# Scores of two 16-head attentions contracted over 32 rows instead of 128, with one copy of the keys

## The chip, the cores and the metric

One core of a Trainium2 chip runs the whole kernel in one launch. The metric is device microseconds (us) of one execution; the profile beside it is one execution taken by the hardware profiler. Engines are called by their short names: PE is TensorE (matmuls; PEld is its weight loads), DVE is VectorE, ACT is ScalarE, POOL is GpSimd, SP issues the DMAs.

## What is computed

Two layers of a small perceiver-like model on x of 4 batch elements, 128 tokens, 128 channels, all in float32. The change touches only the two attentions with 16 heads of 8 channels. The first reads keys from a context of 2048 tokens, of which each head sees every sixteenth, so 128; the second attends over x itself with a relative bias:

```python
# L0_xattn: TK = 2048, head h sees the keys k with (k - h) % 16 == 0, so 128 of them
scores = einsum('bhqd,bhkd->bhqk', Q, K) / sqrt(8)
scores = where((kidx - head) % 16 != 0, -inf, scores)
out = einsum('bhqk,bhkd->bhqd', softmax(scores), V) @ Wo.T + bo
# L1_attn: 128 queries, 128 keys, 16 heads
scores = einsum('bhqd,bhkd->bhqk', q, k) * 8 ** -0.5 + bias(rel. position, head)
out = einsum('bhqk,bhkd->bhqd', softmax(scores), v) @ w_proj.T + b_proj
```

Between them stand a selective-scan layer, a quantised gated MLP, and an attention over the context; behind the second a quantised MLP. Each is preceded by a layer norm and added to x.

## The kernel before, in words

The program is written engine by engine; every engine runs its own fixed list of instructions in order and waits on semaphores. `attention(ph)` stands once in each of the PE, ACT and DVE lists, with ph = 0 for the first 16-head attention and ph = 1 for the second. It is a software pipeline over steps t. In the first 16 steps, step t works on batch element b = t // 4 and on head group g = t % 4 (4 heads each), and one PE bank of PSUM (banks 0 to 2 in turn) holds the 128 queries by 4 x 128 keys of scores.

The channels of q and k lie on the 128 partitions: group g on rows 32g to 32g + 31, and in it head j on 8 rows. PE's score matmuls (L1197 to L1199, recorded at L1089, the helper `mm`) have as stationary operand `q_heads[:, j, ...]`, in which DVE (`queries`, L735 and L738) has multiplied the queries by a mask that keeps the 8 rows of head j in every group. The moving operand is `k_groups[:, g, ...]`: a copy of the keys in which only the 32 rows of group g hold something and the others are zero. So all 128 rows are contracted, and the zeros pick the group. DVE zeroes all of `k_groups` at the start (L857). ACT fills it: `keys(v)` (L431) and `self_keys(b)` (L465) issue four activations of 32 rows for each batch element, one for each group. At the very first batch element each group's copy releases its own step (`k_first`).

One float32 matmul of these is two passes on PE (two records in the trace), a float32 transposition is one. In step t, PE issues: the 4 score matmuls of step t (8 passes of 128 rows by 128 columns); in ph 0, in steps 1 and 2 of four, the key and value projection of the next batch element (`keys_values`, 32 passes that each fill 32 columns of the array); the 4 transpositions of the probabilities of step t - 2 (L1219); and once per batch element a transposition of the inverse sums (L1236, 7 steps after its first), probabilities by values (32 passes of 32 columns, `v_heads`) with a 16-row matmul that spreads the inverse sums (`inv_T`, both 8 steps after it), and the projection (`attn_T`, 10 steps after it). For each step DVE reduces the scores to their maximum (L761; in ph 1 with the bias added, L766) and copies the transposed probabilities (L783), and ACT takes 4 exponentials with their row sums (L483). Scores of step t wait for the step t - 3 to have left its bank and for `k_sb` and `q_heads` of the batch element; transpositions wait for ACT's exponentials.

In ACT's list `keys(b)` stands ahead of the exponentials of steps 3, 7 and 11 of ph 0; `self_keys(b)` ahead of ph 1 for b = 0 and behind the exponentials of steps 1, 4 and 7 for the others.

Of the kernel before, what the change touches and what calls it, by code (L numbers as in the profile page):

```python
# [21 lines left out]
P = 128  # L22
NB = 4
D = 128
T = NB * P
# [70 lines left out]
def two_layers(nc, early, cols, late, rows, ctx_T, taps, ctx, out):  # L96
    st = ExitStack()
    with st:
        def sb(name, shape, dt=F32):
            return st.enter_context(nc.sbuf_tensor(name, shape, dt))  # L100
# [15 lines left out]
        def C(name, i=0, n=1):  # L116
            return cols_sb[:, co[name][0] + i:co[name][0] + i + n]
# [33 lines left out]
        v_T = sb("v_T", [P, P])  # L151
        k_groups = sb("k_groups", [P, NG, T])
        v_heads = sb("v_heads", [P, NB, HG, NG, HG, HD])
# [132 lines left out]
        def turned_xq8(half):  # L286
# [3 lines left out]
            pool_step w_red w_diag w_all w_scaled w_quant bias_vec bias_sb ln_mv ln_rstd xn xnT xnT_sb x_ready  # L290
            xb_ready q_ps q_heads wz kv_ps k_first k_sb vT_sb v_tok_ps v_ps v_sb scores neg_max probs probs_T_ps
            probs_T_sb pv inv_sum invT_ps invT_sb spread_ps o_sb attn proj gates_ps conv_ps w_tap u gate_sb dbc_ps
            bc_hi bc_parts dt_sb dt_ps sp_abs sp_exp delta du du_rest skip a_neg pads k_pads b_ps c_ps c_sb
            decay drive state read y y2 out_ps q_mul q_rnd h_mul h_rnd xq q_gate xqT xqT_sb gate_ps up_ps silu
# [7 lines left out]
        def done(ins, name):  # L302
            return ins.then_inc(S[name], 1)
# [101 lines left out]
        def _(act):  # L405
# [19 lines left out]
            def keys(v):  # L425

                act.wait_ge(S["kv_ps"], 2 * v + 2 if v else 1)
                act.wait_ge(S["k_pads"], 1)
                for g in range(NG):
                    rows = slice(32 * g, 32 * g + 32)  # L430
                    ins = act.activation(k_groups[rows, g, v * P:v * P + P], bank[6][rows, 0:P], ACT.Identity,  # L431
                                         bias=C("bk")[rows, :])
                    if v == 0 and g < NG - 1:
                        done(ins, "k_first")
                done(ins, "k_sb")

# [24 lines left out]
            def self_keys(b):  # L461
                act.wait_ge(S["kv_ps"], 2 * NB + 1 + b // (NB - 1))
                for g in range(NG):
                    rows = slice(32 * g, 32 * g + 32)
                    ins = act.activation(k_groups[rows, g, b * P:b * P + P], bank[6][rows, b * P:b * P + P], ACT.Copy)  # L465
                done(ins, "k_sb")

# [204 lines left out]
        def _(dve):  # L672
# [183 lines left out]
            link(dve.memset(round_col[:, :], ROUND))  # L856
            done(dve.memset(k_groups[:, :, :].rearrange("p g k -> p (g k)"), 0.0), "k_pads")  # L857
            dve.wait_ge(S["early_in"], 16)
# [228 lines left out]
        def _(pe):  # L1087
# [96 lines left out]
            def attention(ph):  # L1184
                w_o = C("woT", 0, D) if ph == 0 else L("w_projT")
                for t in range(NG * (NB - 1) + TURN + 1):
                    if t < 4 * NB:
                        b, g = t // NG, t % NG
                        if ph == 0 and t < NG - 1:
                            pe.wait_ge(S["k_first"], t + 1)  # L1190
                        else:
                            pe.wait_ge(S["k_sb"], ph * NB + b + 1)
                        pe.wait_ge(S["q_heads"], ph * NB + b + 1)
                        if t >= 3:

                            pe.wait_ge(S["probs" if ph == 0 else "neg_max"], ph * 16 + t - 2)
                        for j in range(HG):  # L1197
                            ins = mm(bank[t % 3][:, j * P:j * P + P],
                                     q_heads[:, j, b * P:b * P + P], k_groups[:, g, b * P:b * P + P])  # L1199
                        done(ins, "scores")  # L1200
# [372 lines left out]
```

## Time and profile before

| | us |
|---|---|
| median of 3 runs | 274.31 (274.16 to 276.78) |
| the profiled execution | 275.58 |
| its span, first to last instruction | 273.8 |
| PE busy in it | 208.1 |
| DVE busy | 204.6 |
| ACT busy | 151.7 |
| first 16-head attention (ph 0), scores and what is mixed with them | about 9.7 to 55.8 |
| second 16-head attention (ph 1) | about 206 to 248 |
| mean granted TensorE clock | 0.913 of 2.4 GHz |

The span is what the profile's times are counted in; 1.8 us lie outside it. A granted clock of 1.00 is 2.4 GHz, 0.50 is 1.2 GHz. Busy times of engines overlap; the chain of waits says which one was last at each moment.

### The profile page before, as it was taken

What the parts mean: (1) busy time and instruction counts of PE and PEld (TensorE: products, weight loads), DVE (VectorE), ACT (ScalarE), POOL (GpSimd) and SP (SyncE); (2) the same over time, 40 slices, a digit from 0 to 9 for tenths busy, and PEclk for the clock granted to TensorE, in tenths of its full rate; (3) what the DMA queues carried; (4) which work ended last, traced back from release to release, by engine and by line L of the source; (5) the groups of instructions that cost most, each with busy time, mean ns of one, the idle gap of its engine ahead of it and who ended that gap; (6) DMA issues with size and microseconds to landing.
All of it is one profiled execution on the core that took longest, in us unless ns stands there. A gap on an engine that the chain in (4) does not pass through costs nothing.

```text
span 273.8 us, 4798 instructions
## 1 busy us (share of the span) xinstructions
PE 208.1 (76%) x1561; PEld 140.0 (51%) x1561; DVE 204.6 (75%) x585; ACT 151.7 (55%) x510; POOL 74.8 (27%) x73
## 2 busy tenths in 40 slices
PE   6797897988968777777818778999997699962313
PEld 4676785777622222222303545777876689841102
DVE  5468668832499999999697764687667599985675
ACT  3785957616875555555067655144536699852520
POOL 6013000098037777777880010000010000001000
PEclk9999999999979999999975799999999799995555
DMA  6999800000006884000000023000000000000001
GB/s 236 428 385 414 349 4 0 4 0 2 0 0 70 92 94 52 0 0 2 0 1 1 0 74 81 0 0 2 0 1 2 1 1 2 0 4 0 4 0 38
DMA packets 6745, 16.06 MB, mean 59 GB/s; under 512 B 320, under 2 KB 5056, under 8 KB 5696
## 3 DMA queue, kind: packets, MB, share of 16 engines
q1 hardware_dynamic: 6720, 15.75, 19.9%
q8 instruction: 13, 0.21, 0.3%
q14 instruction: 12, 0.10, 0.1%
HBM read 13.39 MB, written 2.35 MB: 58 GB/s over the span
## 4 chain that ended last, share of the span: by engine, by line
PE 37%; DVE 23%; POOL 15%; issue 11%; ACT 10%; DMA 2%; POOLq 0%; SPq 0%; DVEq 0%; ACTq 0%
PE bank L1089 31%; POOL region L396 15%; ACT probs L483 4%; PE bank L1445 3%; DMA cols_sb<-cols 2%; DVE region L766 2%; DVE region L735 2%; PE bank L1219 2%; DVE region L783 2%; DVE xn L696 1%; DVE stats L691 1%; DVE neg_max L761 1%; ACT k_groups L431 1%; DVE ext L1053 1%; DVE ext L1054 1%
## 5 line engine op out<-in xcount | busy, mean ns | idle before, releaser
L1089 PE MATMUL bank<-region,early_sb 128*128 128x512 f32 x64 | 36.2, 648 | 11.7 <-POOL region L396 11.6
L396 POOL TENSOR_TENSOR region<-region 128x512 f32<-128x512 f32 x32 | 40.6, 1271 | 14.4 <-DVE region L913 14.4
L1089 PE MATMUL bank<-k_groups,region 128*128 128x128 f32 x256 | 36.1, 287 | 4.1 <-ACT k_groups L431 1.5
L913 DVE TENSOR_TENSOR_SCAN region<-region,bank 128x512 f32<-128x512 f32 x32 | 38.5, 1207 | 0.0
L1089 PEld LDWEIGHTS bank<-k_groups,region 128*128 128x128 f32 x256 | 32.2, 198 | 7.0 <-ACT k_groups L431 3.7
L365 POOL TENSOR_TENSOR xb<-x,rows_sb 128x512 f32<-128x512 f32 x3 | 3.8, 1265 | 102.6 <-DVE x L798 43.2
L483 ACT ACTIVATE probs<-bank,neg_max 128x128 f32<-128x128 f32 x64 | 22.6, 366 | 12.0 <-DVE neg_max L761 11.9
L483 ACT ACTIVATE probs<-region,neg_max 128x128 f32<-128x128 f32 x64 | 24.9, 390 | 5.4 <-DVE neg_max L766 5.4
L1089 PEld LDWEIGHTS bank<-region,early_sb 128*128 128x128 f32 x64 | 9.9, 192 | 33.6 <-POOL region L396 33.5
L1089 PE MATMUL bank<-ctx_T_sb,region 128*32 128x128 f32 (+1 forms) x288 | 24.8, 311 | 1.9 <-DVE v_heads L703 1.6
L415 ACT ACTIVATE lnv<-mv,eps_col 128x1 f32<-128x1 f32 x24 | 7.0, 292 | 34.0 <-DVE mv L692 33.8
L783 DVE COPY region<-bank 128x512 f32<-128x512 f32 x32 | 21.8, 682 | 3.8 <-PE bank L1219 3.8
L553 ACT ACTIVATE region<-bank 128x512 f32<-128x512 f32 x16 | 9.5, 595 | 24.2 <-POOL region L396 24.2
L1219 PE MATMUL bank<-early_sb,probs 128*128 128x128 f32 x128 | 20.3, 282 | 2.1 <-ACT probs L483 1.5
L897 DVE TENSOR_TENSOR bank<-region,bank 128x512 f32<-128x512 f32 x32 | 21.4, 672 | 0.0
L567 ACT ACTIVATE region<-region,a_neg 128x508 f32<-128x508 f32 x32 | 21.1, 707 | 0.0
L766 DVE CUSTOM_DVE_ANT_0 region<-bank,region 128x128 f32<-128x128 f32 x64 | 14.5, 283 | 5.3 <-PE bank L1089 5.1
L761 DVE TENSOR_REDUCE neg_max<-bank 128x4 f32<-128x512 f32 x16 | 11.0, 686 | 9.0 <-PE bank L1089 9.0
L1020 DVE COPY region<-bank 128x512 f32<-128x512 f32 x16 | 10.9, 685 | 8.1 <-PE bank L1445 8.1
L1089 PEld LDWEIGHTS bank<-region,ctx_sb 128*128 128x128 f32 x128 | 15.4, 192 | 2.9 <-issue 2.9
L1219 PEld LDWEIGHTS bank<-early_sb,probs 128*128 128x128 f32 x128 | 14.8, 144 | 4.0 <-ACT probs L483 1.9
L1089 PE MATMUL bank<-region,ctx_sb 128*128 128x128 f32 x128 | 15.6, 275 | 0.0
(198 smaller groups left out, 411.5 us busy)
## 6 DMA issues: line engine op xcount, KB each, us to landing
ctx_sb<-ctx SPq DMA_DIRECT2D x4, 1024.0 KB, 24.9
ctx_T_sb<-ctx_T SPq DMA_DIRECT2D x3, 1024.0 KB, 9.8
late_sb<-late SPq DMA_DIRECT2D x1, 2416.0 KB, 18.5
bias_scratch<-bias_vec SPq DMA_DIRECT2D x1, 2040.0 KB, 24.7
ctx_T_sb<-ctx_T SPq DMA_DIRECT2D x2, 512.0 KB, 5.6
region<-bias_scratch SPq DMA_DIRECT2D x1, 1024.0 KB, 5.6
early_sb<-early SPq DMA_DIRECT2D x1, 512.0 KB, 3.6
region<-taps SPq DMA_DIRECT2D x1, 512.0 KB, 19.2
```

Of the source, the lines that this page charges most:

```text
L396: done(pool.tensor_tensor(read[:, k % 3, :], state[:, k % 3, :], c_sb[:, n % 2, :], ALU.mult), "read")
L483: ins = act.activation(probs[:, w % 4, j, :], src[:, j, :], ACT.Exp, bias=neg_max[:, w % 4, j:j + 1], scale=1.0 if ph == 0 else -1.0, accu ...
L553: done(act.activation(c_sb[:, n % 2, :], bank[2][:, :], ACT.Copy), "c_sb")
L567: done(act.activation(dst, src, ACT.Exp, scale=a_neg[:, hf, n:n + 1]), "decay")
L761: done(dve.tensor_reduce(neg_max[:, w % 4, :], src, AX, ALU.max, negate=True), "neg_max")
L766: ins = dve.tensor_tensor_reduce(neg_biased[:, t % 3, j, :], src[:, j, :], rel_bias[:, HG * g + j, :], -1.0, HIGHEST, ALU.add, ALU.min, ne ...
L783: done(dve.tensor_copy(probs_T[:, w % (2 * NG)].rearrange("p h k -> p (h k)"), bank[3 + w % 2][:, :]), "probs_T_sb")
L897: done(dve.tensor_tensor(bank[3 + k % 3][:, :], du[:, hf, :], bank[n % 2][:, :], ALU.mult), "drive")
L913: done(dve.tensor_tensor_scan(state[:, k % 3, :], decay[:, k % NDA, :], bank[3 + k % 3][:, :], 0.0, ALU.mult, ALU.add), "state")
L1020: done(dve.tensor_copy(p2_T[:, w % 4].rearrange("p c q -> p (c q)"), bank[4 + w % 2][:, :]), "p2T_sb")
L1089: return pe.matmul(dst, lhsT, rhs, start=start, stop=stop)
L1219: ins = pe.transpose(bank[3 + w % 2][:, j * P:j * P + P], probs[:, w % 4, j, :], ident)
```

## The change

The tile `k_groups` (4 copies, 3 of 4 rows zero) becomes `k_T`, one copy of the keys with all 128 rows. Its memset and the semaphores `k_pads` and `k_first` go. ACT writes it with one activation of 128 rows for each batch element. The score matmuls read both operands at rows 32g to 32g + 31 only, so that 32 rows are contracted. `q_heads` and its masks are made as before.

```diff
-        k_groups = sb("k_groups", [P, NG, T])
+        k_T = sb("k_T", [P, T])
@@ keys(v)
                 act.wait_ge(S["kv_ps"], 2 * v + 2 if v else 1)
-                act.wait_ge(S["k_pads"], 1)
-                for g in range(NG):
-                    rows = slice(32 * g, 32 * g + 32)
-                    ins = act.activation(k_groups[rows, g, v * P:v * P + P], bank[6][rows, 0:P], ACT.Identity,
-                                         bias=C("bk")[rows, :])
-                    if v == 0 and g < NG - 1:
-                        done(ins, "k_first")
-                done(ins, "k_sb")
+                done(act.activation(k_T[:, v * P:v * P + P], bank[6][:, 0:P], ACT.Identity, bias=C("bk")), "k_sb")
@@ self_keys(b)
                 act.wait_ge(S["kv_ps"], 2 * NB + 1 + b // (NB - 1))
-                for g in range(NG):
-                    rows = slice(32 * g, 32 * g + 32)
-                    ins = act.activation(k_groups[rows, g, b * P:b * P + P], bank[6][rows, b * P:b * P + P], ACT.Copy)
-                done(ins, "k_sb")
+                done(act.activation(k_T[:, b * P:b * P + P], bank[6][:, b * P:b * P + P], ACT.Copy), "k_sb")
@@ DVE, at the start
-            done(dve.memset(k_groups[:, :, :].rearrange("p g k -> p (g k)"), 0.0), "k_pads")
@@ PE, attention(ph), step t
-                        if ph == 0 and t < NG - 1:
-                            pe.wait_ge(S["k_first"], t + 1)
-                        else:
-                            pe.wait_ge(S["k_sb"], ph * NB + b + 1)
+                        pe.wait_ge(S["k_sb"], ph * NB + b + 1)
                         pe.wait_ge(S["q_heads"], ph * NB + b + 1)
@@
+                        rows = slice(32 * g, 32 * g + 32)
                         for j in range(HG):
                             ins = mm(bank[t % 3][:, j * P:j * P + P],
-                                     q_heads[:, j, b * P:b * P + P], k_groups[:, g, b * P:b * P + P])
+                                     q_heads[rows, j, b * P:b * P + P], k_T[rows, b * P:b * P + P])
```

## Rows read from the trace of the kernel before

**Rows 1.** The page: busy time by engine; granted clock in 40 slices, in tenths.
```profile
PE 208.1 (76%) x1561; PEld 140.0 (51%) x1561; DVE 204.6 (75%) x585; ACT 151.7 (55%) x510; POOL 74.8 (27%) x73
...
PEclk9999999999979999999975799999999799995555
```

**Rows 2.** The chain of waits: start us, us, engine and line; key copies in it.
```profile
29.15 0.22 ACT k_groups L431
...
205.71 0.28 ACT k_groups L465
```

**Rows 3.** The tile `k_groups`: engine, operation, count, ns min/median/max, first and last start.
```profile
L1089 PE MATMUL bank<-k_groups,region x256: 275/275/418, 9.7 to 238.8; 128*128 128x128 f32 x128
L431 ACT ACTIVATE k_groups<-bank,cols_sb x16: 342/359/362, 8.5 to 41.5; 32x128 f32<-32x128 f32 x16
L465 ACT ACTIVATE k_groups<-bank x16: 250/268/271, 204.9 to 226.9; 32x128 f32<-32x128 f32 x16
L857 DVE MEMSET k_groups<- x1: 1765/1765/1765, 1.4 to 1.4; 128x2048 f32 x1
```

**Rows 4.** Timeline of DVE, 0 to 10 us: start, us, instruction, idle before.
```profile
4.38 0.29 DVE L691 BATCH_NORM_STATS2 stats<-early_sb 128x6 f32<-128x128 f32 x1 [1.24 <-DMA early_sb<-early]
...
8.23 1.37 DVE L735 TENSOR_SCALAR region<-bank,cols_sb 128x128 f32<-128x128 f32 x4 [1.23 <-DMA cols_sb<-cols]
```

**Rows 5.** Timelines of ACT (28 to 34.5), DVE (203 to 212), PE (212 to 217.5).
```profile
31.90 0.38 ACT L439 ACTIVATE v_T<-bank,cols_sb 128x128 f32<-128x128 f32 x1
...
204.23 1.13 DVE L738 TENSOR_SCALAR region<-bank,cols_sb 128x128 f32<-128x128 f32 x4
...
214.55 1.16 PE L1089 MATMUL bank<-late_sb,xn_T 128*128 128x128 f32 x8 [2.45 <-ACT xn_T L423]
```

**Rows 6.** Timeline of PE, stretches of both attentions; rows*columns of the array used.
```profile
32.65 1.08 PE L1089 MATMUL bank<-region,v_heads 128*32 128x128 f32 x32
33.66 0.48 PE L1089 MATMUL bank<-inv_T,cols_sb 16*128 16x128 f32 x2
34.07 1.16 PE L1089 MATMUL bank<-k_groups,region 128*128 128x128 f32 x8
...
45.42 1.16 PE L1089 MATMUL bank<-k_groups,region 128*128 128x128 f32 x8
...
54.71 0.48 PE L1089 MATMUL bank<-inv_T,cols_sb 16*128 16x128 f32 x2
55.12 0.66 PE L1219 MATMUL bank<-early_sb,probs 128*128 128x128 f32 x4
...
226.92 1.16 PE L1089 MATMUL bank<-k_groups,region 128*128 128x128 f32 x8
227.91 0.60 PE L1219 MATMUL bank<-early_sb,probs 128*128 128x128 f32 x4
228.35 1.06 PE L1089 MATMUL bank<-k_groups,region 128*128 128x128 f32 x8
...
234.62 1.16 PE L1089 MATMUL bank<-k_groups,region 128*128 128x128 f32 x8
```

**Rows 7.** Timeline of PE, 216.8 to 223 us: blocks as in Rows 6.
```profile
216.90 1.06 PE L1219 MATMUL bank<-early_sb,probs 128*128 128x128 f32 x4
217.76 1.81 PE L1089 MATMUL bank<-k_groups,region 128*128 128x128 f32 x8
```

**Rows 8.** Busy us by stretch: PE, PEld, DVE, ACT, POOL, granted clock, DMA.
```profile
21.40:24.80 3.40, 1.74 (x29) 1.58 (x33) 3.40 (x11) 1.51 (x8) 0.13 (x1) 1.00 0.99 414
...
215.90:219.30 3.40, 3.40 (x19) 3.40 (x18) 2.15 (x17) 1.31 (x9) 0.00 (x0) 0.50 0.00 0
...
243.20:246.60 3.40, 2.09 (x37) 1.44 (x37) 2.46 (x10) 0.77 (x3) 0.00 (x0) 1.00 0.01 2
```

**Rows 9.** Timeline of PE: what filled the first and the last stretch of Rows 8.
```profile
21.62 1.11 PE L1089 MATMUL bank<-k_groups,region 128*128 128x128 f32 x8
...
244.99 1.08 PE L1089 MATMUL bank<-region,v_heads 128*32 128x128 f32 x32 [0.36 <-DVE x L798]
```

More of the change, by code:

```diff
@@ L290, in two_layers @@
             pool_step w_red w_diag w_all w_scaled w_quant bias_vec bias_sb ln_mv ln_rstd xn xnT xnT_sb x_ready
-            xb_ready q_ps q_heads wz kv_ps k_first k_sb vT_sb v_tok_ps v_ps v_sb scores neg_max probs probs_T_ps
+            xb_ready q_ps q_heads wz kv_ps k_sb vT_sb v_tok_ps v_ps v_sb scores neg_max probs probs_T_ps
             probs_T_sb pv inv_sum invT_ps invT_sb spread_ps o_sb attn proj gates_ps conv_ps w_tap u gate_sb dbc_ps
-            bc_hi bc_parts dt_sb dt_ps sp_abs sp_exp delta du du_rest skip a_neg pads k_pads b_ps c_ps c_sb
+            bc_hi bc_parts dt_sb dt_ps sp_abs sp_exp delta du du_rest skip a_neg pads b_ps c_ps c_sb
             decay drive state read y y2 out_ps q_mul q_rnd h_mul h_rnd xq q_gate xqT xqT_sb gate_ps up_ps silu
```

## The prediction

> **What bounds the kernel now.** I read the page first, for the shares of the engines and the slices of the granted clock [rows 1]. PE and DVE are each busy three quarters of the span, so the average names no bound; the two stages that the change touches have to be read by themselves. They are ph 0, about 9.7 to 55.8 us, and ph 1, about 206 to 248 us.
>
> Then the chain of waits, for the key copies. In ph 0 the four pieces of `keys(2)` stand in it from 29.15 on and those of `keys(3)` from 40.71 on; in ph 1 those of `self_keys(0)` up to 205.99 [rows 2]. There a whole batch element of scores waits for ACT.
>
> Then the timeline of PE, block by block [rows 6]. Four score matmuls are eight passes, 1.06 from the start of the first to the end of the last, and one lasts 0.275 [rows 3]: they follow each other by 0.112, so a block holds PE for 0.89. Four transpositions take 228.35 - 227.91 = 0.44. PE works one batch element of ph 1 in the 7.70 from 226.92 to 234.62: four steps of 0.89 + 0.44, the values block (33.66 - 32.65 = 1.01), the 16-row pair (34.07 - 33.66 = 0.41), about 0.3 of projection and 0.1 for the inverse sums, 7.1 in all. In ph 0 two blocks of key and value projections of 32 such passes join (1.01 each), so about 9.1 of the 11.35 from 34.07 to 45.42. PE is nearly, but not quite, the bound; DVE and ACT take turns with it.
>
> **What goes.** The memset is 1.765 us of DVE [rows 3], but it begins at 1.4 and DVE then idles 1.24 until the first DMA lands at 4.38 [rows 4]: worth nothing. Without that DMA's cover it would cost its 1.8.
>
> The key copies: four of 0.359 (ph 0) or 0.268 (ph 1), started back to back, fill 1.46 and 1.11 of ACT. The nearest row for one 128-row copy with bias is 0.38 [rows 5]; a 32-row piece takes 0.36 [rows 3], so rows hardly count, and I take 0.38 and 0.28. Gain on ACT: 1.08 for each element of ph 0, 0.83 for each of ph 1. Which of them reach the path:
> - element 0 of ph 0: none. The first scores start at 9.7, behind `queries` on DVE, which starts at 8.23 behind a DMA and takes 1.37 [rows 4]. `k_first` is no loss for the same reason: one copy ends about when its first piece did.
> - element 1: DVE is the last there, busy 3.40 of the 3.40 from 21.40 [rows 8], so little or nothing.
> - elements 2 and 3: 1.08 each, 2.2 together.
> - ph 1, element 0: 0.5. The scores then wait for `queries`, which ends at 205.36 [rows 5], instead of for the copy at 205.99 [rows 2].
> - ph 1, element 1: 0.8, because the copy of `xn_T` that PE waits 2.45 for [rows 5] stands behind it on ACT. Elements 2 and 3: hidden, DVE being busy without a gap.
>
> Without any price on PE that is 3.5 us, and up to 1.7 more if the stretch at half clock at 215.9 [rows 8] does not come because PE idles less ahead of it.
>
> **What is added: changes of the array's shape.** A score pass on 32 rows is not in this trace; the nearest is the 16-row pair [rows 6]. It follows 32-column passes that end at 33.73, and its own two end at 34.14: 0.41, where two passes without a change take 0.22. The scores behind it end at 35.23, 1.09 later instead of 0.89. The transpositions behind the pair at 54.71 end 0.59 later instead of 0.44. So each change costs PE 0.15 (into transpositions) to 0.20. Within the pair the passes are not slower than full ones. I take 32 rows to behave as 16 do; the other bound is no cost at all.
>
> Now the scores have a shape of their own between transpositions. Blocks that stand next to a key projection had a change there already. New ones: into the scores, 11 of the 16 steps in ph 0 and 11 in ph 1, at 0.19; out of them, 10 at 0.15 and one at 0.20 in ph 0, 14 at 0.15 in ph 1. Removed: two at 0.20 in each, where scores follow the 16-row pair. Sum: 3.4 in ph 0 and 3.8 in ph 1, 7.2 us of PE time.
>
> Of this much lies in PE's waits. Carried along the lists in ph 0, PE is 0.35 late after element 0, 0.72 at step 7; the earlier `keys(2)` gives that back up to 0.17, `keys(3)` turns it into a lead of 0.3, and the steps after use this up: net 0.0 at the end of the scores. In ph 1, PE gains about 1.7 up to step 4, but one element now takes 7.1 + 1.0 = 8.1 of PE, more than the 7.7 that the three engines took: the lead shrinks to about 0.9 at step 15, or to nothing if the clock falls at step 4 as before. Queued behind the late scores are DVE's maxima, behind those ACT's exponentials, which release the transpositions of the step after next. On PE's shape changes alone I get 0.4 us faster, 273.9.
>
> **The clock.** This is the term that decides. The granted clock falls to 0.50 (1.2 GHz) at 215.9 [rows 8], and again from slice 37 of the page, 246.4, to the end [rows 1]. Before the second fall PE was busy 2.09 us of 3.40. In the equal stretch from 21.40 it was busy only 1.74, and the clock stayed at 1.00 there and in the next slices [rows 1]. What differs is what filled them [rows 9]: eight passes on the whole array in the one; passes on 32 columns, the 16-row pair and a 16-column transposition in most of the other. So busy time alone does not keep the clock; passes on a part of the array appear to hold it up less. The change turns the largest group of whole-array passes of both stages, 256 [rows 3], into passes on a quarter of its rows, beside the same narrow value and key passes. In ph 1 the first three steps are only such passes, 2.9 us of them between two waits.
>
> The Trainium skill, in "TensorE: Matmul & The Clock Gate", Part 1, says that the gate follows how busy PE has been recently. By that alone nothing would fall, PE being busier than before, and the time would be the first rival's. The two stretches above do not agree with busy time as the only measure, though two stretches are thin evidence.
>
> The price of the lower clock is in the rows: scores that take 0.89 take 1.64 (217.76 to the next block at 219.40), transpositions that take 0.44 take 0.86 (216.90 to 217.76) [rows 7]. A step costs 1.17 more; the values block, the pair and the rest about 1.5 more an element; in ph 0 the projections 2.0 more. At half clock throughout, PE needs 8.1 + 6.2 = 14.3 for an element of ph 1 and 10.1 + 8.2 = 18.3 for one of ph 0. Against 7.7 and 11.35 that is 6.6 and 7.0 later, 54 us over eight elements. No row says for how much of the stages the clock stays down. Ends: one fall, which costs half its length, 1.7, and all of it, 54. Transpositions and key projections, which stay whole-array or four abreast, can bring it back in ph 0; in the old trace PE was busy all of 215.90 to 219.30 before it came back. I take half: 27. With -0.4 from above: 274.3 + 26 = **300 us**. The sum is made against the profiled execution, 275.6 with a span of 273.8, which lies 1.3 over the median; the difference is then put on the median.
>
> **The rivals.**
> 1. *Clock untouched.* Changes of shape eat what the copies give: 273.9, 272 to 277. For it: the skill's rule, and that the old trace held the clock through sparse parts of ph 0. Against it: rows 8 and 9.
> 2. *Faster: 32-row passes change the array's shape for free*, or groups on different rows overlap. Then the 3.5 us of copies come through, perhaps with the fall at 215.9: 269 to 271. It decides if the transpositions behind a score block start 0.11 after its last pass, not 0.20. Against it: both neighbours of the 16-row pair. For it: nothing but that 16 is not 32. The skill ("TensorE: Matmul & The Clock Gate", Part 3) lets small-K matmuls run at once only on distinct row groups; here the four heads of a step share one. Overlap could come only between steps 0, 1 and 2 of ph 1, well under 1 us.
> 3. *The slower clock in ph 1 only*: there PE has no key projections to hold it. 4 x 6.6 = 26 at most, half of it 13: 287. This is inside my forecast's own range.
>
> **Chances.** Clock falls for much of the stages: 0.60, its own range 280 to 318. Clock untouched, within 1%: 0.25. Changes of shape cost more on the path than I found, over 1% slower without the clock: 0.04. Faster: 0.11. Faster or slower means by over 1% (2.7 us), about what a measurement of this kernel can tell from no change. The range runs from 272.5, which takes in nearly all of rival 1, to 318.
>
> **What would show it.** In the chain: no `k_T` piece over 0.4 us. Timeline of PE: 0.20 from the last transposition to the first score pass, about 1.09 for a score block. Clock by stretch: values of 0.5 between 10 and 56 us and from about 209 on; score blocks of 1.7 us there. Wrong if the clock reads 1.00 through both stages: then 274; wrong the other way if nothing lies between blocks: then 270. ACT should lose 4.3 + 3.3 = 7.6 us of busy time less pipelining, whatever else happens.

## The result, and the profile after

| | us |
|---|---|
| with the change, median of 4 executions | 294.74 (285.68 to 304.52) |
| before, beside them | 275.47 (274.16 to 276.78) |
| ratio | 1.043 [1.0349, 1.051] |
| with the change, 4 more executions on another chip | 287.74 (285.34 to 300.09) |
| before, 13 executions beside those | 276.65 (274.03 to 279.9) |

The change makes the kernel slower. The ratio is about 12 us (0.043 x 275.5). The forecast of 300 was 25.7 above the time before; by the ratio less than half of that came, and the median of the first four lies 19 above before, inside the range. The eight executions with the change spread over 19 us where those before spread over 3 to 6, and the ratio is taken from the shorter ones only, so it gives the least that the change costs.

Two executions were profiled, one of 304.5 us and one of 285.8, and I read both. The page of the longer one, busy time by engine and granted clock in 40 slices (before: [rows 1]):

```profile
span 302.7 us, 4769 instructions
...
PE 244.1 (81%) x1559; PEld 164.2 (54%) x1561; DVE 204.5 (68%) x584; ACT 144.6 (48%) x486; POOL 74.8 (25%) x73
...
PEclk9998599857989999999986799999965555695555
```

The page of the shorter one:

```profile
span 284.0 us, 4771 instructions
...
PE 223.9 (79%) x1561; PEld 148.2 (52%) x1561; DVE 203.4 (72%) x584; ACT 144.0 (51%) x486; POOL 74.7 (26%) x73
...
PEclk9557799968998999999996679999999599995555
...
PE 46%; DVE 20%; POOL 14%; issue 10%; ACT 5%; DMA 2%; POOLq 0%; SPq 0%; DVEq 0%; ACTq 0%
```

DVE does what it did, ACT is 7.1 to 7.7 us less busy, and PE is 36 and 16 us more busy with as many instructions: the same passes last longer. The longer execution has 5s and 6s in slices 30 to 35, in the second attention; the shorter one has a 5 there in slice 32 alone. That makes most of the difference of the two. The last line is the shares of the chain by engine: PE rose from 37% to 46% (52% in the longer one).

The tile that replaced `k_groups`, shorter execution (before: [rows 3]):

```profile
L1078 PE MATMUL bank<-k_T,region x256: 269/270/577, 9.9 to 248.9; 32*128 32x128 f32 x128
L428 ACT ACTIVATE k_T<-bank,cols_sb x4: 367/378/378, 9.1 to 48.8; 128x128 f32<-128x128 f32 x4
L456 ACT ACTIVATE k_T<-bank x4: 253/255/277, 215.6 to 235.9; 128x128 f32<-128x128 f32 x4
```

One copy of 128 rows takes 0.378 and 0.255, and a score pass is as short as before, 0.270, where the clock is at its upper level; its longest is 0.577.

Stretches of the shorter execution: busy us of PE, PEld, DVE, ACT, POOL, then the granted clock, DMA:

```profile
9.90:24.80 14.90, 14.87 (x129) 11.21 (x129) 3.75 (x9) 6.07 (x32) 1.29 (x2) 0.50 0.99 406
31.60:35.10 3.50, 3.50 (x39) 2.78 (x40) 1.03 (x2) 1.50 (x8) 0.00 (x0) 0.51 0.40 162
58.90:65.80 6.90, 6.90 (x53) 5.24 (x52) 4.46 (x15) 2.89 (x16) 1.47 (x2) 0.51 0.01 2
219.40:226.20 6.80, 6.09 (x26) 5.32 (x26) 4.95 (x26) 5.70 (x30) 0.00 (x0) 0.50 0.01 2
226.20:252.00 25.80, 25.04 (x259) 20.70 (x259) 24.04 (x146) 20.71 (x103) 0.00 (x0) 1.00 0.01 2
```

The same first stretch of the kernel before:

```profile
9.90:24.80 14.90, 12.49 (x182) 10.38 (x185) 10.41 (x30) 10.55 (x53) 1.40 (x2) 1.00 1.00 402
```

Before, those 14.9 us were at 2.4 GHz and PE started 182 matmuls in them. Now they are at 1.2 GHz, PE has no gap left, and starts 129; DVE is busy 3.75 instead of 10.41, because it waits for scores (10.3 us of waits for PE). The same in the second attention of the longer execution:

```profile
221.90:262.80 40.90, 39.82 (x213) 33.11 (x214) 24.57 (x140) 22.17 (x110) 0.00 (x0) 0.50 0.00 1
```

Where the time is, by stage, from the first score to the last x of each attention (start and end read from the timelines of PE and DVE):

| | first attention | second | together |
|---|---|---|---|
| before | 53.7 | 42.2 | 95.9 |
| change, shorter execution | 64.6 | 42.1 | 106.7 |
| change, longer execution | 67.3 | 58.0 | 125.3 |

The other stages keep their lengths: 106.7 - 95.9 = 10.8 against 10.2 between the spans, 29.4 against 28.9.

### The profile page after: what moved, and what is told of

Same layout as the page of the kernel before. It is cut to its first block, busy times and chain, and to the rows that moved or that the text cites. A ratio compares the mean times of both kernels' runs of the same rounds, so it can differ in the third digit from the quotient of the medians.

```text
span 302.7 us, 4769 instructions
## 1 busy us (share of the span) xinstructions
PE 244.1 (81%) x1559; PEld 164.2 (54%) x1561; DVE 204.5 (68%) x584; ACT 144.6 (48%) x486; POOL 74.8 (25%) x73
## 4 chain that ended last, share of the span: by engine, by line
PE 52%; DVE 18%; POOL 13%; issue 9%; ACT 5%; DMA 1%; POOLq 0%; another core or an unknown queue 0%; DVEq 0%; ACTq 0%
PE bank L1078 41%; POOL region L396 13%; PE bank L1206 7%; PE bank L1432 2%; DVE region L725 1%; DMA early_sb<-early 1%; DVE region L773 1%; PE bank L1097 1%; DVE xn L686 1%; DVE stats L681 1%; DVE neg_max L751 1%; DVE ext L1042 1%; ACT probs L473 1%; DVE ext L1043 1%; DVE region L949 1%
## 5 line engine op out<-in xcount | busy, mean ns | idle before, releaser
L1078 PE MATMUL bank<-k_T,region 32*128 32x128 f32 x256 | 50.0, 357 | 1.2 <-DVE region L728 0.7
L1078 PEld LDWEIGHTS bank<-k_T,region 32*128 32x128 f32 x256 | 42.7, 253 | 8.9 <-issue 5.9
L1078 PE MATMUL bank<-region,early_sb 128*128 128x512 f32 x64 | 36.0, 644 | 12.7 <-POOL region L396 12.6
L1206 PE MATMUL bank<-early_sb,probs 128*128 128x128 f32 x128 | 28.4, 361 | 2.1 <-ACT probs L473 1.6
L1078 PE MATMUL bank<-ctx_T_sb,region 128*32 128x128 f32 (+1 forms) x288 | 29.1, 392 | 0.9 <-DVE v_heads L693 0.6
L1078 PEld LDWEIGHTS bank<-region,early_sb 128*128 128x128 f32 x64 | 9.5, 188 | 34.5 <-POOL region L396 34.5
L1206 PEld LDWEIGHTS bank<-early_sb,probs 128*128 128x128 f32 x128 | 18.2, 178 | 8.1 <-issue 4.3
L1078 PEld LDWEIGHTS bank<-ctx_T_sb,region 128*32 128x32 f32 (+1 forms) x288 | 14.3, 151 | 5.1 <-issue 2.8
L1009 DVE COPY region<-bank 128x512 f32<-128x512 f32 x16 | 10.9, 685 | 8.1 <-PE bank L1432 8.1
```

Source lines behind the costliest of these rows:

```text
L1009: done(dve.tensor_copy(p2_T[:, w % 4].rearrange("p c q -> p (c q)"), bank[4 + w % 2][:, :]), "p2T_sb")
L1078: return pe.matmul(dst, lhsT, rhs, start=start, stop=stop)
L1206: ins = pe.transpose(bank[3 + w % 2][:, j * P:j * P + P], probs[:, w % 4, j, :], ident)
```

## Experiments

The diffs are against the kernel before where nothing else is said; lines that stay as they are are left out, and of the longest three (`three_row_groups_once`, `pairs_on_two_row_groups`, `pool_spreads_keys`) only the main lines are shown. "Before" is the kernel before beside the run. Of all kernels but the two that say so the whole model is computed.

### Which part costs: the copies or the 32 rows

`rows_only_pe`: the padded copies, their memset and `k_first` stay; only PE reads 32 rows.

```diff
+                        rows = slice(32 * g, 32 * g + 32)
-                                     q_heads[:, j, b * P:b * P + P], k_groups[:, g, b * P:b * P + P])
+                                     q_heads[rows, j, b * P:b * P + P], k_groups[rows, g, b * P:b * P + P])
```

> The kernel before with its four zero-padded key copies left as they are; only the score matmuls read rows 32g to 32g+31 of both operands. Theory (the 32-row passes cost the time, through the clock and the changes of shape): as slow as the changed kernel or up to 4 us slower, 286 to 306 us, long stretches at granted clock 0.50 in both attentions. Rival (the single copy, or the dropped first-key hand-over, has to do with the loss): near 274 us.

Measured: 299.07 (before 277.57), ratio 1.0784 [1.0727, 1.084]. The 32 rows are what costs, and without the copies' gain they cost more: 3.5% more than the change, about 10 us, of which the copies explain 4.4 (the next run). The rest is not attributed; executions with 32-row scores differ by more than that. The trace of this run, of an execution of 320.1 us, shows a granted clock of 0.85 where the others show 1.00 (190 to 230 us, for one); no number is taken from it.

`one_copy_128_rows`: the change with its scores contracted over all 128 rows of `k_T`. This sums the scores of four groups, so the output is not the reference's; the work and its order are those of the change.

```diff
 (against the change)
-                        rows = slice(32 * g, 32 * g + 32)
+                        rows = slice(0, P)
```

> The changed kernel, but the score matmuls contract all 128 rows of the single key copy, so each score sums over the four head groups and the output is not the reference's; same number of passes, copies and waits as the change. Theory: no new shape on PE and no fall of the clock beyond those of before; what is left is the gain of the copies, 3.5 us or, if the fall at 215.9 goes too, up to 5: 269 to 271 us. Rival (the clock falls because the lists wait differently, whatever the rows): above 280 us.

Measured: 272.67 (before 277.57), ratio 0.9841 [0.9788, 0.9895], 4.4 us faster. Its granted clock, 40 slices:

```profile
PEclk9999999999977999999995999999999999985555
```

The fall that stood in slice 32 before [rows 1] is gone. So the copies give what they were to give (4.4 us, interval 2.9 to 5.9), and one slice of rows turns 1.6% faster into 4.3% slower.

`scores_64_rows`: the same with 64 rows (two groups summed, so not the reference's output either).

> The changed kernel with scores contracted over the 64 rows of two groups (each score sums two groups, so the output is not the reference's). The changes of shape on PE are as many as with 32 rows. Theory (how much of the array a pass uses is what keeps the clock up): the clock falls for less time than with 32 rows, 275 to 284 us. Rival (the gaps of the changes of shape bring the clock down): same as with 32 rows, 286 us or more. Second rival (only whole-array passes count): same as with 32 rows too.

Measured: 293.83, from 280.24 to 318.65 in four executions, mean granted clocks 0.903 to 0.711. One of the four lies in the 275 to 284 that I expected. 64 rows do not keep the clock up in every execution either; the spread is too wide to set 64 between 32 and 128, and what makes it this wide stays open.

### Does it need the attention at all

`warmers_32_rows`: the kernel before already issues 64 filler matmuls of `ones` (`keep_warm`), the first 20 while it waits for its first data, the others in later stages. Here these alone read 32 rows; the attentions are untouched.

```diff
-                    mm(bank[at][:, 0:2 * P], ones[:, :].bitcast(BF16)[:, 0:P], ones[:, :].bitcast(BF16))
+                    mm(bank[at][:, 0:2 * P], ones[0:32, :].bitcast(BF16)[:, 0:P], ones[0:32, :].bitcast(BF16))
```

> The kernel before; only the idle-time filler matmuls on ones (64 of them, their results are never read) use 32 instead of 128 rows. They last as long and PE is as busy. Theory: they no longer bring or hold the clock up; passes at half clock at the start of the first attention, and the stretches behind the fillers at 0.50 for longer: 277 to 290 us, with a wider spread between executions. Rival (busy time alone counts): 274 us, granted clock 0.91 as before.

Measured: 282.72 (before 277.57), ratio 1.0201 [1.0143, 1.0258]. The mean granted clock of its four executions is 0.879 to 0.890, that of the seven before 0.909 to 0.925. The two spans differ by 7.8 us. The first attention grows by 2.4 us to 56.1 and the second stays at 42.2; 4.8 us lie between them, where 44 of the fillers are issued: from the last x of the first attention to the first score of the second it takes 147.4 instead of 142.6. The change's two profiles have 141.6 and 141.8 there, `one_copy_128_rows` 140.5. Busy time and granted clock of the stretch around and behind the last fillers, in this run and then before:

```profile
155.40:169.10 13.70, 12.07 (x55) 6.96 (x56) 7.12 (x25) 5.74 (x17) 1.26 (x1) 0.50 0.24 67
```

```profile
157.90:175.00 17.10, 14.11 (x76) 8.94 (x75) 10.93 (x25) 7.49 (x26) 1.27 (x1) 1.00 0.24 62
```

The start of the kernel looks like evidence too, and is none. Timeline of PE, this run:

```profile
0.98 4.44 PE L1089 MATMUL bank<-ones 32*128 32x256 bf16 x20 [0.98 <-POOL ones L347]
...
10.26 2.00 PE L1089 MATMUL bank<-k_groups,region 128*128 128x128 f32 x8 [0.53 <-ACT k_groups L431]
```

The same start of the kernel before:

```profile
0.98 3.96 PE L1089 MATMUL bank<-ones 128*128 128x256 bf16 x20 [0.98 <-POOL ones L347]
...
9.74 1.13 PE L1089 MATMUL bank<-k_groups,region 128*128 128x128 f32 x8 [1.39 <-DVE region L735]
```

And of `one_copy_128_rows`, whose fillers use the whole array:

```profile
0.97 4.45 PE L1078 MATMUL bank<-ones 128*128 128x256 bf16 x20 [0.97 <-POOL ones L347]
...
10.38 2.07 PE L1078 MATMUL bank<-k_T,region 128*128 128x128 f32 x8 [0.55 <-ACT k_T L428]
```

With fillers on 32 rows, passes are spaced as at the upper level only from 12.0 on instead of 4.3, and the first block of scores, on 128 rows both times, takes 2.00 instead of 1.13. But with whole-array fillers the third kernel starts as slowly. One start in one execution tells nothing about rows. The reading rests on the time and the mean clock of all four executions and on the stretch between the attentions. Only the number of rows that the filler passes use was changed, so this is the cleanest of the runs on the cause.

### Shape changes without the clock

`column_tiles_whole_array`: the scores of a head as four tiles of 32 columns of the array, each on all 128 rows of the padded copies. The shape now changes at the transpositions as often as in the change, but the four tiles together fill the array.

```diff
                         for j in range(HG):
+                            for c in range(4):
+                                ins = mm(bank[t % 3][32 * c:32 * c + 32, j * P:j * P + P],
+                                         q_heads[:, j, b * P + 32 * c:b * P + 32 * c + 32],
+                                         k_groups[:, g, b * P:b * P + P])
```

> The kernel before, its padded keys and 128 contracted rows kept, but each score matmul split into four of 32 queries that fill 32 columns of the array each, four abreast. The score blocks last about as long (32 passes, 1.0 us) and change the array's shape as often as the changed kernel, while the whole array is in use. If the loss is the clock's: granted clock as before and at most 2 us slower than before. If the loss is the changes of shape: 8 us slower or more, near the changed kernel.

Measured: 278.4 in 10 executions (before 276.65 in 13), ratio 1.0074 [1.0034, 1.0113], 2.0 us slower. Timeline of PE in the second attention, and the clock:

```profile
228.47 1.08 PE L1089 MATMUL bank<-k_groups,region 128*32 128x128 f32 x32
229.48 0.66 PE L1221 MATMUL bank<-early_sb,probs 128*128 128x128 f32 x4
230.07 1.08 PE L1089 MATMUL bank<-k_groups,region 128*32 128x128 f32 x32
...
PEclk9599999999957999999995999999999799998555
```

1.01 for the scores (229.48 - 228.47) and 0.59 for the transpositions, as often as in the change and nearly as long (1.60 a step, in the change 1.67, before 1.33). The clock stays up through both attentions but for the start, 7.1 to 13.9, which `pool_spreads_warmed` below has too in slice 2 with its whole-array scores, and a dip in slice 32 that the kernel before has. So changing the shape costs about 2.0 us here, interval 0.9 to 3.1, and the change has a quarter more of it (0.34 a step against 0.27). `one_copy_128_rows` and the change, 1.6% faster and 4.3% slower, lie 16 us apart; what the changes of shape leave of that, 10 us and more, is the clock.

### Which attention

`rows_first_attention` and `rows_second_attention`: as `rows_only_pe`, in one attention each.

```diff
+                        rows = slice(32 * g, 32 * g + 32) if ph == 0 else slice(0, P)    # the other run: ph == 1
```

> The kernel before, with 32-row scores in the first attention only (key copies as before). Key projections of 32 columns, four abreast, run beside them and hold the clock in part. Theory: 5 to 12 us slower than before, falls of the clock between 10 and 60 us, ph 1 as before. Rival (only the second attention matters, as it has no projections to hold the clock): within 4 us of before.

> The kernel before, with 32-row scores in the second attention only (key copies as before). Theory: one long stretch at granted clock 0.50 from about 210 us to the end of the stage, 10 to 16 us slower. With the first-attention run the sum of both losses is that of the rows-only kernel (about 22 us). Rival (losses are all in the first): within 4 us of before.

Measured: 289.61, ratio 1.042 [1.0325, 1.0514]; and 284.96, ratio 1.0321 [1.0252, 1.0391] (before 275.87). Together 7.4%, near the 7.8% of both at once. The first, 11.6 us by its ratio, lies in what I expected; the second, 8.9, is short of its 10 to 16, and its clock came back ahead of the end of the stage. The clock of the first run, then of the second:

```profile
PEclk9877599956997999999998697999999899999555
```

```profile
PEclk9999999999799999999959999999975558996555
```

Beside falls that the kernel before has too (slices 12, 21 to 23, 32, and the end [rows 1]), the clock is down where the 32-row scores are: in slices 2 to 5, 9 and 10 of the first run (stages 66.0 and 42.7 us), in slices 30 to 34 of the second (53.7 and 50.9; at the lower level from 206.7 to 234.0).

### Buying the clock back

`change_plus_2_warmers` and `change_plus_4_warmers`: the change, and ahead of each score block two or four filler matmuls on the whole array, in the bank that the scores then overwrite.

```diff
 (against the change)
+                        keep_warm(4, t % 3)
                         rows = slice(32 * g, 32 * g + 32)
```

> The changed kernel with 2 more filler matmuls (whole array, bf16, 0.11 us each at full clock; their result is overwritten) ahead of each of the 32 score blocks: 7 us of PE work that computes nothing. Theory (the change costs through the clock, and the clock falls because too little of the array is in use): the work added makes the kernel faster than the changed one, ratio to before 1.01 to 1.03, and the executions spread less. Rival (PE is simply the bound through its changes of shape): slower than the changed kernel by up to 7 us.

> As with 2 fillers, but 4 for each score block, 14 us of PE work. Theory: the clock stays at 1.00 through both attentions, executions agree within 1%; PE is then the bound by its own work, ratio to before 1.02 to 1.04. This also shows the price of the changes of shape with the clock held. Rival (PE bound by changes of shape, clock no matter): 14 us slower than the changed kernel, ratio 1.09 or more.

Measured: 296.87 (289.84 to 301.77), and 302.43, ratio 1.0894 [1.0813, 1.0974] (before 275.87). With four fillers the kernel is slower than the change (1.043); with two, its 289.84 to 301.77 lie among the change's 285.34 to 304.52 and are not told apart from them. Neither came near the 1.01 to 1.03 and 1.02 to 1.04 that I expected. Timeline of PE with four fillers:

```profile
25.66 0.60 PE L1078 MATMUL bank<-ones 128*128 128x256 bf16 x4
26.19 1.15 PE L1078 MATMUL bank<-k_T,region 32*128 32x128 f32 x8
27.27 0.66 PE L1207 MATMUL bank<-early_sb,probs 128*128 128x128 f32 x4
```

In this profile the clock was up from 17.8 to 58.8, longer than in either profile of the change, and the mean clocks of the four executions are 0.851 to 0.888 where the change has 0.807 to 0.862 in eight: fillers raise the mean clock. They do not hold it. With two of them it was down from 26.5 to 43.6, and with four the second attention still fell, from 222.6 to 246.5. And PE has no wait to put them in: blocks follow each other and each step is 0.53 longer (26.19 - 25.66). I had taken it that the fillers would pay for themselves; they cost 0.53 x 32 = 17 us at the upper level alone.

`before_warmed`: the kernel before, with 16 fillers in the wait of 2.45 [rows 5].

```diff
                     if ph == 1 and t == LAST_TURN + 1:
+                        keep_warm(16, (t + 1) % 3)
                         self_values()
```

> The kernel before with 16 whole-array fillers (1.8 us) in the 2.45 us for which PE waits at 212 to 214.5 us. Theory: what PE does ahead of it decides on the fall at 215.9 us; it goes, and the scores behind it take 1.06 instead of up to 1.8 us: 1 to 1.7 us faster. Rival (the fall moves to the next thin stretch, or DVE sets the pace anyway): within 0.5 us of before.

Measured: 274.4 in 12 executions (before 276.5 in 29), ratio 0.9945 [0.99, 0.9989]. Its clock has no fall in slice 32:

```profile
PEclk9999999999958999999995999999999999997555
```

In a real gap fillers cost nothing, and the run is 1.5 us faster (interval 0.3 to 2.8), where I had put 1 to 1.7 on the fall. That the gain is that fall rests on this one profile, in which the second attention takes 41.1 instead of 42.2.

### Do 32-row passes overlap

The second profile of the change, `change_again`, was taken for the parts that do not hang on the clock, beside the two runs that follow.

> The changed kernel itself once more, beside the other three on one chip, for comparison and for a second profile. Theory: 284 to 305 us, the execution with the higher mean clock the faster; the first attention hit or missed depending on when the clock falls.

Measured: 287.74 (285.34 to 300.09), as in the table above; the mean clocks of the two shorter executions are 0.856 and 0.862, of the two longer 0.846 and 0.807.

`three_row_groups_once`: the scores of steps 0, 1 and 2 of the second attention, which wait for nothing between them, issued head by head: one matmul on each of three row groups in turn.

```diff
 (against the change)
+                    if ph == 1 and t == 0:
+                        for j in range(HG):
+                            for s in range(3):
+                                rows = slice(32 * s, 32 * s + 32)
+                                ins = mm(bank[s][:, j * P:j * P + P], q_heads[rows, j, 0:P], k_T[rows, 0:P])
```

> The changed kernel; only the scores of the first three steps of the second attention, which have nothing between them, are issued in turn on three row groups: 24 passes. If row groups overlap: the block takes 1.0 to 1.3 us instead of 2.9 at full clock (2.0 to 2.6 instead of 5.5 at half), time as the changed kernel. If not: as the changed kernel in both.

Measured: 301.78 (290.31 to 312.04), ratio 1.056 [1.0423, 1.0696]. The time says only that the clock fell again. The question is answered by the block itself, first in this run, then in the change:

```profile
221.06 1.17 PE L1078 MATMUL bank<-k_T,region 32*128 32x128 f32 x24 [0.67 <-DVE region L728]
```

```profile
216.28 2.23 PE L1078 MATMUL bank<-k_T,region 32*128 32x128 f32 x24 [0.67 <-DVE region L728]
```

Twenty-four passes in 1.17, where one after the other they would take 24 x 0.112 = 2.7: three row groups run abreast. Even in the change's order, eight passes on one group and then eight on the next, 24 take 2.23.

`pairs_on_two_row_groups`: steps t and t + 1 issued together, alternating between two row groups, through both attentions.

```diff
 (against the change)
+                        for j in range(HG):
+                            for s in (t, t + 1):
+                                g = s % NG
+                                rows = slice(32 * g, 32 * g + 32)
+                                ins = mm(bank[s % 3][:, j * P:j * P + P],
+                                         q_heads[rows, j, b * P:b * P + P], k_T[rows, b * P:b * P + P])
```

> The changed kernel with the scores of steps t and t + 1 issued together at even t, pass by pass on two different row groups in turn. If passes on different row groups overlap, a pair takes about 1 us instead of 2 x 1.1, PE loses half of its changes of shape too, and the kernel is faster than the changed one, 275 to 290 us. If they do not overlap: near the changed kernel, or slower since scores come in bursts.

Measured: 281.88 (280.37 to 282.6; before 276.65), ratio 1.0194 [1.0112, 1.0276]. Two blocks of this run, at the lower and at the upper clock:

```profile
26.63 2.08 PE L1078 MATMUL bank<-k_T,region 32*128 32x128 f32 x16
...
38.25 1.16 PE L1078 MATMUL bank<-k_T,region 32*128 32x128 f32 x16
```

Sixteen passes now take what eight took (2.07, 1.15), and the kernel is faster than the change on the same chip (280.37 to 282.6 against 285.34 and up) although its clock is no better (mean 0.845; the change's two profiles have 0.821 and 0.862). Overlap shortens the work but does not save the clock, and it stays slower than before.

### A version that beats both

`pool_spreads_keys`: PE's 128 rows and the padded copies as before, but ACT makes one 128-row copy and POOL, idle at that time, spreads it into the four (not for the first batch element of each attention). Each spread group releases its own step.

```diff
+            def spread_keys(v):
+                pool.wait_ge(S["k_copied"], v - v // NB)
+                b = v % NB
+                for g in range(NG):
+                    rows = slice(32 * g, 32 * g + 32)
+                    done(pool.tensor_copy(k_groups[rows, g, b * P:b * P + P], k_T[rows, :]), "k_sb")
```

> The kernel before with 128-row scores and padded keys kept; for all batch elements but the first of each attention, ACT makes one 128-row copy of the keys and POOL, which idles there, spreads it over the four padded copies, each group released by itself. Theory (what the single copy brings is ACT time, about 1.1 us an element, and whole-array passes cost nothing): 2 to 4 us faster than before. Rival (the scores wait for POOL's copies, slower than ACT's, or POOL and DVE get in each other's way): same as before or slower.

Measured: 273.17 in 12 executions (before 276.5 in 29), ratio 0.9928 [0.9884, 0.9972]. POOL's timeline, and the clock:

```profile
18.73 1.32 POOL L374 COPY k_groups<-k_T 32x128 f32<-32x128 f32 x4 [13.17 <-ACT k_T L448]
...
PEclk9999999999989999999995999999999999985555
```

Four copies take POOL 1.32 at a time when it had idled 13 us, ACT is relieved (145.6 us busy instead of 151.7 [rows 1]), and PE keeps its 128 rows and its clock. This keeps 2.0 us (interval 0.8 to 3.2) of the 4.4 that the single copy gives with 128 rows, and leaves the loss.

`pool_spreads_warmed`: this with ten fillers ahead of `self_values()`.

> As the POOL version, with 10 whole-array fillers (1.1 us) where PE waits for the last transposed xn in the second attention, ahead of the fall of the clock at 215.9 us. Theory: the fall goes, and with it up to 1.7 us: 4 to 5 us faster than before. Rival (the fall is no longer there, or comes elsewhere): as without fillers.

Measured: 273.73, ratio 0.9918 [0.9883, 0.9953], the same within its interval: in the profile without fillers the fall at 215.9 had already gone (PE's wait there is 1.33 instead of 2.45), so there was nothing left to buy.

## Why the prediction was right in kind and wrong in size

**What goes.** The copies are 0.378 and 0.255 where I took 0.38 and 0.28, and ACT lost 7.7 us in the shorter profile where I had 7.6. With 128 rows they were worth 4.4 us, between the 3.5 without and the 5.2 with the fall at 215.9 [rows 8]. That fall did go in the run with 128 rows; in the change's shorter execution it did not, and lasted from 219.4 to 226.2.

**Shape changes.** Timeline of PE of the shorter execution in the second attention (before: [rows 6]):

```profile
229.49 1.15 PE L1078 MATMUL bank<-k_T,region 32*128 32x128 f32 x8
230.57 0.66 PE L1206 MATMUL bank<-early_sb,probs 128*128 128x128 f32 x4
...
235.45 1.08 PE L1078 MATMUL bank<-region,v_heads 128*32 128x128 f32 x32
236.46 0.37 PE L1078 MATMUL bank<-inv_T,cols_sb 16*128 16x128 f32 x1
236.47 0.37 PE L1078 MATMUL bank<-k_T,region 32*128 32x128 f32 x1
...
236.68 0.94 PE L1078 MATMUL bank<-k_T,region 32*128 32x128 f32 x7
237.55 0.66 PE L1206 MATMUL bank<-early_sb,probs 128*128 128x128 f32 x4
238.14 1.15 PE L1078 MATMUL bank<-k_T,region 32*128 32x128 f32 x8
...
244.50 0.37 PE L1078 MATMUL bank<-k_T,region 32*128 32x128 f32 x1
```

A score block holds PE for 1.08 (230.57 - 229.49) and the transpositions for 0.59 (238.14 - 237.55), which are the 0.89 + 0.20 and 0.44 + 0.15 of the forecast. One element takes 8.03 (236.47 to 244.50), forecast 8.1, before 7.70. Taking 32 rows to behave as 16 do was right. Behind the 16-row pair there is no change, as I had it, and more: the first score pass starts 0.01 behind the first of the pair. On the path the changes cost 2.0 (0.9 to 3.1) in `column_tiles_whole_array`; the forecast had turned -3.5 into -0.4, so 3.1. That run's changes are a fifth shorter, and it keeps ACT's late copies, so that PE's waits for them can cover some of the cost; how much was not measured.

The Trainium skill, "TensorEngine Tiling (Array Packing)", says under its key properties that switching the tiling mode drains the array; these rows show a cost at each switch, 0.15 to 0.20 us, which agrees. The Trainium skill, "TensorE: Matmul & The Clock Gate", Part 3, lets matmuls on distinct row groups run at once; 24 passes in 1.17 us agree.

**The clock.** The cause was right, and the two stretches of the old trace pointed to it [rows 8]: passes on part of the array do not keep the clock up as passes on all of it do. `warmers_32_rows` shows it with no other change, `column_tiles_whole_array` shows that the shape change is not it, and `one_copy_128_rows` that nothing else in the change is. The Trainium skill, "TensorE: Matmul & The Clock Gate", Part 1, lets the clock follow how busy PE has been. By that alone `warmers_32_rows` should have been no slower, its fillers being as many and as long (median 416 ns, before 417); it was 2.0% slower, so the measurement decides against busy time as the only measure.

**The step that failed is "I take half: 27".** It is the fraction of the two stages that the clock spends at its lower level. In the shorter execution the first attention has 14.9 + 3.5 + 6.9 = 25.3 us at 0.50, in which PE is busy throughout and so loses about half, 12.6. The copies give 2.2 of it back: 10.4, measured 10.9 (64.6 - 53.7). In the second attention 6.8 us at 0.50 lose about 3.4; the 3.4 us at 0.50 of the kernel before [rows 8] had lost half of that already, and the copies pay for most of the rest: 42.1 against 42.2. So about 16 of the 54 were lost, not 27. In the longer execution the two attentions grew by 13.6 + 15.8 = 29.4, 3 more than the 26 of the forecast, because the second was at 0.50 for 40.9 us on end; with the 3.5 of the copies added back that is some 33 of the 54. The fraction was a guess between bounds 52 us apart, and it is not one number: it differs from execution to execution. That the median of the first four came within 6 us of the forecast is luck. (The sum, 274.3 - 0.4 + 27, also makes 300.9; I wrote 26 and 300.)

The price of the lower clock was sized right. In the longer execution one batch element of the second attention takes 261.87 - 247.17 = 14.70 at 0.50 throughout, forecast 14.3:

```profile
247.17 0.58 PE L1078 MATMUL bank<-k_T,region 32*128 32x128 f32 x1
...
261.87 0.58 PE L1078 MATMUL bank<-k_T,region 32*128 32x128 f32 x1
```

**What stays open** is why one execution keeps the clock in the second attention and another does not, with the same instructions in the same order. The runs show only the two outcomes, and that the clock also comes back during 32-row scores: from 226.20 on it is at 1.00 with PE busy 25.04 of 25.80. Open too is how much of the array, rows between 32 and 128, is enough; and whether the narrow value and key passes beside the scores have a part in the falls.

**The rivals.** The first, clock untouched at 273.9, is out: no execution was under 285. The second, faster, had its condition wrong (0.20 lies ahead of a score block, not 0.11) and its side remark held for the change's own order only: I gave overlap of row groups "well under 1 us" on steps 0 to 2, and it is 0.7 there, from 2.94 before to 2.23; issued in turn it is 1.8. The third, slower clock in the second attention only, is out: the first attention by itself loses 4.2% (the second 3.2%; the intervals overlap). Key projections and transpositions do not hold the clock there as I thought they might. Chances of 0.60 for the falling clock and 0.64 for slower stand well against that; 273.9 at 0.25 leaned on a rule of busy time that the old trace already spoke against.

## What to carry to other kernels

Contracting over fewer rows saves nothing on a pass (0.270 on 32 rows, 0.275 on 128) and can cost the clock, so zeros that fill the array may be cheaper than a slice; if the copies are what hurts, move them to an idle engine. Where small slices are needed, issue them in turn over row groups, and put fillers only where PE waits anyway. Price a step that may move the clock as a share of the stage at each level, and expect executions to differ.

## What the runs showed that I had not expected

- Three row groups run abreast with float32 operands: 24 passes in 1.17 us, 16 on two groups in 1.16, against 8 on one group in 1.15.
- Passes of a 16-row and a 32-row tile overlap (236.46 and 236.47), although their numbers of rows differ.
- A POOL copy of 32 x 128 float32 takes 0.286 us from start to end and four follow in 1.32, less than ACT's four of 0.359 with their 1.46.
- The granted clock can be shown too high. In the longer execution the view gives the stretch below as 1.00, but eight passes take 2.07 in it, and 1.15 later; the starts of `warmers_32_rows` and `one_copy_128_rows` are shown so too. Where the two disagree, the spacing of passes is the better witness. Window, then timeline:

```profile
9.90:20.50 10.60, 10.23 (x85) 7.41 (x86) 1.72 (x4) 4.63 (x24) 1.27 (x1) 1.00 0.98 407
...
10.27 2.07 PE L1078 MATMUL bank<-k_T,region 32*128 32x128 f32 x8 [0.55 <-ACT k_T L428]
...
23.11 1.15 PE L1078 MATMUL bank<-k_T,region 32*128 32x128 f32 x8
```
